# A graph network on one core: first layer ahead of the edge ranks, index work moved into the first blocks, padding rows scattered by GpSimd

## Chip, cores and metric

The kernel runs on one NeuronCore of a Trainium2 chip. The metric is the device time of one execution in microseconds (us). Engines are named TensorE (PE in the profile; PEld is its weight load), VectorE (DVE), ScalarE (ACT), GpSimd (POOL) and SyncE (SP), the last of which issues most DMA transfers.

## What is computed

Two graph layers follow each other on 512 nodes of 256 features, with 16,384 edges. The first carries nearly all of the work: three dense layers on every edge, then a sum over the edges of each source node, then a dense part on the nodes. The second layer is node attention, messages along the same edges, a feed-forward part and a gated unit.

```python
m = gelu(h_E @ m0_w + m0_b)          # 16384 x 512 -> 256
m = gelu(m @ m1_w + m1_b)            # 256 -> 256
m = gelu(m @ m2_w + m2_b)            # 256 -> 256
dh = segment_sum(m, src_idx, num_segments=512) / 30.0
h = layer_norm(h_V + dh)
d = gelu(h @ d0_w + d0_b); d = gelu(d @ d1_w + d1_b); d = d @ d2_w + d2_b
x = layernorm(x + layer_norm(h + d))
...
msg = x1[dst] * x1[src]
attn_out = segment_sum(msg, dst, num_segments=512)
```

## The kernel before

**Edge blocks.** The edges are taken in 32 blocks of 512 (`NBLK`, `BLK`). `layer_0(b, m)`, `layer_1(b)` and `layer_2(b)` are TensorE's three layers of block b. Every float32 product is made of three passes over values split into a rounded part and its rest (`x_hi`, `x_lo`): ScalarE rounds (`round_x`), VectorE subtracts (`rest_x`, `rest_w`, `rest_0`, `rest_1`). TensorE's order in block b is `layer_1(b)`, `layer_0(b + 1, 0)`, `layer_2(b)`, `layer_0(b + 1, 1)`. VectorE adds the last bias (`biased`), ScalarE applies the last gelu (`gelu_2`) into `m2`.

**Sorting the edges.** To sum over source nodes, the rows of `m2` are sorted by source group (128 nodes each, `NC` = 4 groups) through HBM. Blocks are taken in 8 sorts (`SORT_BLOCKS`: six of 4 blocks, two of 3). A sort owns a stretch of the HBM tensor `sorted_rows`, in which each group begins on a multiple of 128 rows. GpSimd writes the rows with indirect DMAs (L450, four of 128 rows for each block) at the addresses in `place`. For the last two blocks (`DIRECT`) no sort is made. Rows of `sorted_rows` that get no edge must hold -1 in their index columns, so SyncE first fills each sort's whole stretch from the tile `no_edge` (`fill`, L363), ahead of the scatters. `fill(0)` is issued behind the loads of blocks 0 to 2, the others in blocks 1, 5, 9 and so on to 25. GpSimd waits for the fill (`filled`) at the first block of a sort.

**Summing.** The sorted rows come back in chunks of 5 tiles of 128 rows (`reload(q)`, L374, into `sorted_raw`), from block 4 on. VectorE makes one-hot matrices of their index columns (`hot_src`, `hot_dst`; the latter's first one of a chunk stands between `rest_1(b, 0)` and `rest_1(b, 1)`), ScalarE and VectorE split the values (`round_sorted`, `rest_sorted`), and `sum_sorted(q)` adds them up on TensorE, 6 blocks behind (`LAG_SUM`).

**The index work ahead of it.** `group_edges` (VectorE) makes `group_hot`, the group of each edge as one-hot; `rank_edges` (TensorE, L1262 and L1264) counts with 17 matmuls how many edges of the same group stand ahead; `place_edges` (VectorE) turns that into addresses, group beginnings (`group_at`) and the group of each tile (`tile_group`). TensorE runs `rank_edges`, then 16 warming matmuls on the identity (`keep_warm`, L1317), then `layer_0(0, ...)`. Each engine carries out its program in the order in which it is written; there is no scheduler. All DMAs that SyncE issues share one queue, in the page q1. In block 26 SyncE loads the node weights of the next stage (`x_rows`, `d0_w`, and `d1_w` of 4 MB).

VectorE's order before block 0 was:

```python
group_edges()
for g in range(2):
    rest_w(g)
    rest_x(0, g)
rest_w(2)
rest_w(3)
place_edges()
rest_0(0, 0)
```

## Time and profile before

| | us |
|---|---|
| median of 3 timed runs | 628.16 (627.64 to 629.81) |
| the profiled execution | 624.47 |
| its span, first to last instruction | 622.7 |
| TensorE busy | 591.8 (95%) |
| VectorE busy | 458.0 (74%) |
| ScalarE busy | 366.5 (59%) |
| GpSimd busy | 193.1 (31%) |
| moved by DMA | 102.82 MB, of which 35.53 MB written to HBM |
| mean granted clock of TensorE | 0.994 |

The span runs from the first to the last instruction; the execution's own time is 1.8 us longer. TensorE's matmuls are pipelined, and each one's end is modelled, so differences of starts are read rather than durations. A wait is shown in brackets behind an instruction: how long its engine was idle ahead of it, and what released it. The granted clock is 1.00 at 2.4 GHz and 0.50 at 1.2 GHz.

### The profile page before, as it was taken

To read this page: it belongs to the slowest core of one execution; us is meant where nothing else is said; L and a number is where in the kernel's file an instruction comes from. 1 tells how busy PE (TensorE), PEld (TensorE's weight loads), DVE (VectorE), ACT (ScalarE), POOL (GpSimd) and SP (SyncE) were. 2 spreads that over 40 slices of the span, in tenths; PEclk is the share of its full clock that TensorE was granted. 3 is DMA by queue.
4 is the path that set the end of the run, shared out by engine and by line. 5 is a ranking of instruction groups with operands and counts; after the bars stand their busy time and mean duration, and the time that the engine had idled before them with its cause. 6 is when DMAs were issued, how large, how long until landed. Compare 5 with 4: busy or idle time off the path is not lost.

```text
span 622.7 us, 9161 instructions
## 1 busy us (share of the span) xinstructions
PE 591.8 (95%) x3273; PEld 507.7 (82%) x3273; DVE 458.0 (74%) x781; ACT 366.5 (59%) x554; POOL 193.1 (31%) x182
## 2 busy tenths in 40 slices
PE   4999999999999999999999989998789999999895
PEld 1888887898888888888888978888778889778673
DVE  4756577778778887787887869879546666778567
ACT  4667686776777767776777766663156352420341
POOL 3035345534554445543554344510000010100001
PEclk9999999999999999999999999999799999999999
DMA  7994399499479549739748994232021213000000
GB/s 245 286 280 168 116 284 321 122 274 288 146 229 304 192 128 280 254 108 284 241 153 232 354 397 147 80 119 86 1 102 68 101 44 136 1 0 2 0 1 34
DMA packets 51483, 102.82 MB, mean 165 GB/s; under 512 B 3568, under 2 KB 41328, under 8 KB 46960
## 3 DMA queue, kind: packets, MB, share of 16 engines
q1 hardware_dynamic: 45104, 86.04, 44.6%
q0 software_dynamic: 5760, 15.92, 7.7%
q8 instruction: 28, 0.46, 0.3%
q10 hardware_dynamic: 576, 0.28, 0.2%
q14 instruction: 15, 0.12, 0.1%
HBM read 66.69 MB, written 35.53 MB: 164 GB/s over the span
## 4 chain that ended last, share of the span: by engine, by line
PE 81%; DMA 9%; DVE 6%; issue 2%; ACT 2%; POOL 1%; SPq 0%; POOLq 0%; ACTq 0%; DVEq 0%
PE ps L1209 24%; PE ps L1245 8%; DMA sorted_raw<-sorted_rows 7%; PE ps L1391 7%; PE ps L1251 4%; PE ps L1227 4%; PE ps L1223 4%; PE ps L1222 4%; PE ps L1359 3%; PE ps L1290 3%; PE ps L1294 3%; PE ps L1292 3%; PE ps L1432 2%; PE ps L1317 2%; PE ps L1402 2%
## 5 line engine op out<-in xcount | busy, mean ns | idle before, releaser
L450 POOL DMA_INDIRECT sorted_rows<-m,place x120 | 163.1, 1359 | 211.3 <-ACT m L514 182.8
L497 ACT ACTIVATE m_hi<-ps,cols 128x512 fp32r<-128x512 f32 x128 | 88.3, 690 | 75.7 <-PE ps L1209 47.5
L772 DVE TENSOR_TENSOR m_lo<-m_out,m_hi 128x512 fp32r<-128x512 f32 x128 | 88.7, 693 | 59.1 <-ACT m_out L499 55.7
L1209 PE MATMUL ps<-x_hi,w_hi 128*128 128x512 f32 x256 | 100.2, 391 | 0.0
L1209 PE MATMUL ps<-x_lo,w_hi 128*128 128x512 f32 x256 | 100.1, 391 | 0.0
L1209 PE MATMUL ps<-x_hi,w_lo 128*128 128x512 f32 x256 | 99.8, 390 | 0.0
L499 ACT ACTIVATE m_out<-ps,cols 128x512 f32<-128x512 f32 x128 | 88.0, 688 | 0.0
L688 DVE TENSOR_TENSOR x_lo<-x_raw,x_hi 128x1024 fp32r<-128x1024 f32 x64 | 75.8, 1224 | 7.0 <-ACT x_hi L491 7.0
L1245 PE MATMUL ps<-w_lo,m_hi 128*128 128x256 f32 x256 | 64.2, 283 | 0.0
L1245 PE MATMUL ps<-w_hi,m_hi 128*128 128x256 f32 x256 | 64.0, 282 | 0.0
L491 ACT ACTIVATE x_hi<-x_raw 128x1024 fp32r<-128x1024 f32 x62 | 62.2, 1058 | 1.9 <-DMA x_raw<-in_edges_dram 1.9
L514 ACT ACTIVATE m<-m_in 128x512 f32<-128x512 f32 x64 | 39.5, 634 | 40.4 <-DVE m_in L785 40.4
L803 DVE TENSOR_SCALAR pack_hot<-iota,sorted_raw 128x256 fp32r<-128x256 f16 x144 | 53.4, 408 | 7.3 <-DMA sorted_raw<-sorted_rows 7.3
L1209 PEld LDWEIGHTS ps<-x_hi,w_lo 128*128 128x128 f32 x256 | 48.1, 188 | 10.3
L1209 PEld LDWEIGHTS ps<-x_hi,w_hi 128*128 128x128 f32 x256 | 48.2, 188 | 9.2
L1209 PEld LDWEIGHTS ps<-x_lo,w_hi 128*128 128x128 f32 x256 | 48.2, 188 | 8.8
L785 DVE TENSOR_TENSOR m_in<-ps,m2b 128x512 f32<-128x512 f32 x64 | 41.2, 686 | 19.1 <-PE ps L1251 19.1
L1245 PEld LDWEIGHTS ps<-w_lo,m_hi 128*128 128x128 f32 x256 | 49.0, 192 | 1.2
L1223 PE MATMUL ps<-m_hi,w_lo 128*128 128x512 f32 x128 | 50.0, 390 | 0.0
L1245 PEld LDWEIGHTS ps<-w_hi,m_hi 128*128 128x128 f32 x256 | 48.9, 191 | 1.2
L1222 PE MATMUL ps<-m_hi,w_hi 128*128 128x512 f32 x128 | 49.9, 390 | 0.0
L1290 PE MATMUL ps<-sorted_hi,src_hot 128*128 128x256 f32 x144 | 42.9, 298 | 5.8 <-issue 3.8
(208 smaller groups left out, 1140.7 us busy)
## 6 DMA issues: line engine op xcount, KB each, us to landing
x_raw<-in_edges_dram SPq DMA_DIRECT2D x31, 1024.0 KB, 7.3
sorted_raw<-sorted_rows SPq DMA_DIRECT2D x24, 647.5 KB, 5.2
sorted_rows<-no_edge SPq DMA_DIRECT2D x6, 2460.5 KB, 19.3
d_w<-in_d_dram SPq DMA_DIRECT2D x1, 4096.0 KB, 27.8
sorted_rows<-no_edge SPq DMA_DIRECT2D x2, 1942.5 KB, 17.0
sorted_raw<-sorted_rows SPq DMA_DIRECT2D x6, 518.0 KB, 4.0
rows<-in_rows_dram SPq DMA_DIRECT2D x1, 2176.0 KB, 8.3
d_w<-in_d_dram SPq DMA_DIRECT2D x2, 1024.0 KB, 11.4
```

Source lines behind the costliest of these rows:

```text
L450: pool.indirect_dma_start(out=sorted_d, out_offset=bass.IndirectOffsetOnAxis(ap=place[:, at:at + 1], axis=0), in_=m2[:, b % 2, t], in_offs ...
L491: nc.scalar.activation(x_hi[:, b % 2, K_HALF[h]], x_raw[:, b % 2, K_HALF[h]], ACT.Copy).then_inc(x_hi_done, 1)
L497: nc.scalar.activation(out_hi[:, m], ps[:, bank], ACT.Gelu, bias=col(bias, m)).then_inc(hi_signal, 1)
L499: nc.scalar.activation(m_out[:, m], ps[:, bank], ACT.Gelu, bias=col(bias, m)).then_inc(signal, 1)
L688: nc.vector.tensor_tensor(x_lo[:, b % 2, ks], x_raw[:, b % 2, ks], x_hi[:, b % 2, ks].bitcast(F32), ALU.subtract).then_inc(x_lo_done, 1)
L772: nc.vector.tensor_tensor(lo[:, m], m_out[:, m], hi[:, m].bitcast(F32), ALU.subtract).then_inc(done, 1)
L803: nc.vector.tensor_scalar(pack_hot[:, q % 2, t], iota[:, 0:2 * P], near, unit, ALU.is_equal, ALU.mult)
L1209: last = nc.tensor.matmul(out, left, right, start=(k == 0 and i == 0), stop=(k == KE - 1 and i == 2))
L1222: nc.tensor.matmul(out, w(1, k, m, w_hi), m0_hi[:, k], start=(k == 0), stop=False, skip_group_check=True)
L1223: nc.tensor.matmul(out, w(1, k, m, w_lo), m0_hi[:, k], start=False, stop=False, skip_group_check=True)
L1245: nc.tensor.matmul(out, m1_hi[:, k, e], part[:, at:at + H], stop=False, skip_group_check=True, start=(k == 0 and part is w_hi and t % 2 == 0))
L1290: nc.tensor.matmul(group_sum[:, g], hot, sorted_hi[:, q % 2, t], start=False, stop=False, skip_group_check=True)
```

## The change

It has five parts.

- **TensorE's start.** The warming matmuls come first, as soon as the identity is there; then `layer_0(0, 0)` and `layer_0(0, 1)`; `rank_edges` stands behind them, ahead of `layer_1(0)`.
- **VectorE's start.** The first halves of weights and input of block 0 are split ahead of `group_edges`.
- **Index work.** `place_edges` is cut into `count_groups` (block 0, behind the input of block 2), `place_edges` (end of block 0) and `group_tiles` (end of block 1).
- **Padding.** The eight fills are gone. A new `pad_rows` (VectorE, end of block 2) computes the addresses of the rows that get no edge, 384 for each sort, and GpSimd scatters `no_edge` into them: 24 indirect DMAs of 128 rows, two in each block from block 3 to 14, ahead of the block's own scatters. `reload` waits for a sort's three (`padded`) at its first chunk, the load of `d1_w` for all of them, `sum_sorted(0)` for their addresses.
- **Drain.** A `drain` of GpSimd follows its last scatter.

```diff
+PADS = NC - 1
...
+        FIRST_PADS = 3
...
-
-            def fill(s):
-                rows_s = sorted_d[s * TILES * P:(s * TILES + SORT_TILES[s]) * P].rearrange("(t p) f -> p t f", p=P)
-                all_rows = no_edge[:].rearrange("p (a f) -> p a f", a=1).to_broadcast([P, SORT_TILES[s], ROW])
-                sp.dma_start(rows_s, all_rows).then_inc(filled[s], 16)
 
...
@@ -368,6 +372,7 @@
                     past = SORT_FIRST[sort] + SORT_BLOCKS[sort]
                     for par in range(2):
                         sp.wait_ge(scattered[par], 64 * ((past + 1 - par) // 2))
+                    sp.wait_ge(padded[sort], 16 * PADS)
                 if q >= 2:
                     sp.wait_ge(sorted_ready, q - 1)
                 at = (sort * TILES + CHUNK * c) * P
...
             load_x(1)
             load_x(2)
-            sp.wait_ge(consts, 1)
-            fill(0)
             for b in range(NBLK):
                 if b + 3 < NBLK:
                     load_x(b + 3)
-                if b % 4 == 1 and b // 4 + 1 < SORTS:
-                    fill(b // 4 + 1)
                 if b == NBLK - 6:
                     sp.dma_start(x_rows[:].rearrange("p c f -> p (c f)"), x_rows_d).then_inc(early_loaded, 16)
                     sp.dma_start(d0_w[:].rearrange("p a b -> p (a b)"), d0_d).then_inc(early_loaded, 16)
-                    sp.wait_ge(placed, 1)
+                    for s in range(SORTS):
+                        sp.wait_ge(padded[s], 16 * PADS)
                     sp.dma_start(d1_w[:].rearrange("p a b -> p (a b)"), d1_d).then_inc(early_loaded, 16)
...
                 if b == 0:
                     pool.wait_ge(placed, 1)
                 pool.tensor_copy(m2[:, b % 2, :, H:ROW], edge_id[:, b * TB:(b + 1) * TB]).then_inc(ids_in, 1)
-                if b in SORT_FIRST:
-                    pool.wait_ge(filled[SORT_FIRST.index(b)], 16)
+                if b == FIRST_PADS:
+                    pool.wait_ge(pads_placed, 1)
+                for i in range(max(2 * (b - FIRST_PADS), 0), min(2 * (b - FIRST_PADS) + 2, PADS * SORTS)):
+                    rows_at = pad_place[:, i // PADS, i % PADS:i % PADS + 1]
+                    pool.indirect_dma_start(out=sorted_d, out_offset=bass.IndirectOffsetOnAxis(ap=rows_at, axis=0),
+                                            in_=no_edge[:], in_offset=None).then_inc(padded[i // PADS], 16)
                 pool.wait_ge(ids_in, b + 1)
                 for t in range(TB):
                     pool.wait_ge(gelu2, 2 * b + t // 2 + 1)
                     at = place_of(b, t)
                     pool.indirect_dma_start(out=sorted_d, out_offset=bass.IndirectOffsetOnAxis(ap=place[:, at:at + 1], axis=0),
                                             in_=m2[:, b % 2, t], in_offset=None).then_inc(scattered[b % 2], 16)
+            pool.drain()
...
-            def place_edges():
+            def count_groups():
 
                 totals = ps[:, CNT].rearrange("p (g s c) -> p g s c", g=NC, s=SORTS)
-                ranks = ps[:, CNT + 1].rearrange("p (g s c) -> p g s c", g=NC, s=SORTS)
                 dve.wait_ge(ranked, 1)
                 dve.wait_ge(consts, 2)
                 idx(nc.vector.tensor_reduce(group_n[:], totals, AX_X, ALU.add))
...
+                row_s = sort_row[:].rearrange("p (a s) -> p a s", a=1).to_broadcast([P, NC, SORTS])
+                idx(nc.vector.scalar_tensor_tensor(group_row[:], group_at[:], float(P), row_s, ALU.mult, ALU.add))
+                idx_wait()
+
+            def group_tiles():
+
                 one = slice(0, 1)
                 for g in (1, 2, 3):
...
-                row_s = sort_row[:].rearrange("p (a s) -> p a s", a=1).to_broadcast([P, NC, SORTS])
-                idx(nc.vector.scalar_tensor_tensor(group_row[:], group_at[:], float(P), row_s, ALU.mult, ALU.add))
                 idx_wait()
                 idx(nc.vector.tensor_tensor(tile_past[one, 0], tile_past[one, 0], tile_past[one, 1], ALU.add))
+                idx_wait()
+                idx(nc.vector.tensor_tensor(tile_group[one], tile_past[one, 0], tile_past[one, 2], ALU.add))
+
+            def place_edges():
+
+                ranks = ps[:, CNT + 1].rearrange("p (g s c) -> p g s c", g=NC, s=SORTS)
                 first = group_row[:].rearrange("p g (s a) -> p g s a", a=1).to_broadcast([P, NC, SORTS, COLS_SORT])
                 idx(nc.vector.tensor_tensor(rank[:], ranks, first, ALU.add))
                 idx_wait()
-                idx(nc.vector.tensor_tensor(tile_group[one], tile_past[one, 0], tile_past[one, 2], ALU.add))
                 idx(nc.vector.tensor_tensor(rank[:], rank[:], group_hot[:, :, :, COLS_SORT - 1:], ALU.mult))
...
                 idx_wait()
                 idx(nc.vector.tensor_reduce(place_f[:], rank[:].rearrange("p g s c -> p (s c) g"), AX_X, ALU.add))
                 idx_wait()
                 nc.vector.tensor_copy(place[:], place_f[:]).then_inc(placed, 1)
+
+            def pad_rows():
+
+                idx(nc.vector.tensor_copy(before_n[:, 0], group_n[:, 0]))
+                idx_wait()
+                for g in range(1, PADS):
+                    idx(nc.vector.tensor_tensor(before_n[:, g], before_n[:, g - 1], group_n[:, g], ALU.add))
+                    idx_wait()
+                idx(nc.vector.scalar_tensor_tensor(before_n[:], group_at[:, 1:], float(P), before_n[:], ALU.mult, ALU.subtract))
+                idx_wait()
+                each = [P, PADS, SORTS, PADS]
+                limit = before_n[:].rearrange("p g (s a) -> p g s a", a=1).to_broadcast(each)
+                rows_in = group_n[:, 1:].rearrange("p g (s a) -> p g s a", a=1).to_broadcast(each)
+                idx(nc.vector.tensor_tensor(pad_past[:], pad_no[:].to_broadcast(each), limit, ALU.is_ge))
+                idx(nc.vector.tensor_tensor(pad_row[:], pad_row[:],
+                                            group_n[:, 0].rearrange("p (s a) -> p s a", a=1).to_broadcast([P, SORTS, PADS]),
+                                            ALU.add))
+                idx_wait()
+                idx(nc.vector.tensor_tensor(pad_past[:], pad_past[:], rows_in, ALU.mult))
+                idx_wait()
+                idx(nc.vector.tensor_reduce(pad_n[:], pad_past[:].rearrange("p g s k -> p s k g"), AX_X, ALU.add))
+                idx_wait()
+                nc.vector.tensor_tensor(pad_place[:], pad_row[:], pad_n[:], ALU.add).then_inc(pads_placed, 1)
 
             def rest(hi, lo, signal, done, b, m):
 
@@ -840,13 +882,13 @@
                 into = count[:, 2 * r:2 * r + 2, far * H:(far + 1) * H]
                 nc.vector.tensor_tensor(into, into, field.rearrange("p (g n) -> p g n", g=2), ALU.add).then_inc(count_step, 1)
 
+            rest_w(0)
+            rest_x(0, 0)
+            rest_w(1)
             group_edges()
-            for g in range(2):
-                rest_w(g)
-                rest_x(0, g)
+            rest_x(0, 1)
             rest_w(2)
             rest_w(3)
-            place_edges()
             rest_0(0, 0)
             rest_x(1, 0)
             rest_x(1, 1)
...
@@ -857,6 +899,8 @@
                 if b + 2 < NBLK:
                     rest_x(b + 2, 0)
                     rest_x(b + 2, 1)
+                if b == 0:
+                    count_groups()
                 for s, first in enumerate(COUNTS_OUT_AT):
                     if first <= b < first + 4:
                         add_counts(s, (b - first) // 2, (b - first) % 2)
@@ -872,6 +916,12 @@
                 rest_0(b + 1, 0)
                 biased(b, 0)
                 biased(b, 1)
+                if b == 0:
+                    place_edges()
+                if b == 1:
+                    group_tiles()
+                if b == 2:
+                    pad_rows()
                 if q >= 0:
                     for t in range(2, CHUNK):
                         hot_dst(q, t)
@@ -1256,7 +1306,6 @@
             def rank_edges():
 
                 pe.wait_ge(group_ready, 1)
-                pe.wait_ge(ident_ready, 1)
                 flat = group_hot[:].rearrange("p g s c -> p (g s) c")
                 own = flat[:, :, COLS_SORT - 1:]
                 nc.tensor.matmul(ps[:, CNT], all_ones[:], own, start=True, stop=True)
@@ -1273,7 +1322,7 @@
 
                 sort, c, n = CHUNKS[q]
                 if q == 0:
-                    pe.wait_ge(placed, 1)
+                    pe.wait_ge(pads_placed, 1)
                     clear(SUM)
                     clear(SUM + 1)
                 if q == 0 or q - 1 in COUNT_AFTER:
@@ -1316,10 +1365,11 @@
                 for _ in range(products):
                     nc.tensor.matmul(ps[:, bank, 0:P], ident[:], ident[:], start=True, stop=True)
 
-            rank_edges()
+            pe.wait_ge(ident_ready, 1)
             keep_warm(16, 0)
             layer_0(0, 0)
             layer_0(0, 1)
+            rank_edges()
             for b in range(NBLK - 1):
                 layer_1(b)
                 layer_0(b + 1, 0)
```

VectorE before its first block, in the kernel before from the end of `group_edges` on (names: `w_lo`, `x_lo` are the rests of weights and input, `part_i`, `group_hot` and `edge_id` come from `group_edges`, `group_n` is the first of `place_edges`):

```order
L726 CAST direct_src<-src_i 128x8
L727 CAST iota<-iota_i 128x512
L728 CAST edge_id<-part_i 128x128
L729 CAST edge_id<-part_i 128x128
L730 TENSOR_SCALAR edge_id<-part_i 128x128
L693 TENSOR_TENSOR w_lo<-w_raw,w_hi 128x512 [waits w_hi_done]
L688 TENSOR_TENSOR x_lo<-x_raw,x_hi 128x1024 [waits x_hi_done]
L693 TENSOR_TENSOR w_lo<-w_raw,w_hi 128x512 [waits w_hi_done]
L688 TENSOR_TENSOR x_lo<-x_raw,x_hi 128x1024 [waits x_hi_done]
L693 TENSOR_TENSOR w_lo<-w_raw,w_hi 128x512 [waits w_hi_done] x2
L739 TENSOR_REDUCE group_n<-ps 128x32 [waits consts,ranked]
```

and VectorE's first rows in the changed kernel:

```order
L704 TENSOR_TENSOR w_lo<-w_raw,w_hi 128x512 [waits w_hi_done]
L699 TENSOR_TENSOR x_lo<-x_raw,x_hi 128x1024 [waits x_hi_done]
L704 TENSOR_TENSOR w_lo<-w_raw,w_hi 128x512 [waits w_hi_done]
L722 TENSOR_SCALAR part_i<-src_i 128x128 [waits idx_loaded]
L723 TENSOR_SCALAR part_i<-src_i 128x128
L724 TENSOR_SCALAR part_i<-dst_i 128x128
L725 TENSOR_SCALAR part_i<-dst_i 128x128
L733 TENSOR_SCALAR group_hot<-part_i 128x6x16 [waits idx_step,consts]
```

and, VectorE still, behind the middle of `group_edges`:

```order
L738 CAST iota<-iota_i 128x512
L739 CAST edge_id<-part_i 128x128
L740 CAST edge_id<-part_i 128x128
L741 TENSOR_SCALAR edge_id<-part_i 128x128
L699 TENSOR_TENSOR x_lo<-x_raw,x_hi 128x1024 [waits x_hi_done]
L704 TENSOR_TENSOR w_lo<-w_raw,w_hi 128x512 [waits w_hi_done] x2
L814 TENSOR_TENSOR m_lo<-m_out,m_hi 128x512 [waits gelu0]
```

The first two rests of the weights and the first half of the input's have moved ahead of the edge groups, and m_lo follows the weights directly, with no index work between.

VectorE at the end of block 0 in the changed kernel (`m_in` is `biased`, `m_lo` behind it is `rest_0(1, 1)`):

```order
L814 TENSOR_TENSOR m_lo<-m_out,m_hi 128x512 [waits gelu1]
L814 TENSOR_TENSOR m_lo<-m_out,m_hi 128x512 [waits gelu0]
L827 TENSOR_TENSOR m_in<-ps,m2b 128x512 [waits l2_done] x2
L780 TENSOR_TENSOR rank<-ps,group_row 128x512
L782 TENSOR_TENSOR rank<-rank,group_hot 128x512 [waits idx_step]
L784 TENSOR_REDUCE place_f<-rank 128x128 [waits idx_step]
L786 CAST place<-place_f 128x128 [waits idx_step]
L814 TENSOR_TENSOR m_lo<-m_out,m_hi 128x512 [waits gelu0]
L699 TENSOR_TENSOR x_lo<-x_raw,x_hi 128x1024 [waits x_hi_done] x2
```

The four operations from `rank` to `place` have come in between `m_in` and `m_lo`, which stood next to each other.

SyncE's queue from the load of block 1 on, before:

```order
L358 DMA x_raw<-in_edges_dram 128x2048
L358 DMA x_raw<-in_edges_dram 128x2048 [waits x_lo_done]
L363 DMA sorted_rows<-no_edge 128x19x259 [waits consts]
L358 DMA x_raw<-in_edges_dram 128x2048 [waits x_lo_done] x2
L363 DMA sorted_rows<-no_edge 128x19x259
L358 DMA x_raw<-in_edges_dram 128x2048 [waits x_lo_done] x3
L374 DMA sorted_raw<-sorted_rows 128x5x259 [waits scattered1,scattered0]
L358 DMA x_raw<-in_edges_dram 128x2048 [waits x_lo_done]
L363 DMA sorted_rows<-no_edge 128x19x259
L374 DMA sorted_raw<-sorted_rows 128x5x259
```

and now:

```order
L367 DMA x_raw<-in_edges_dram 128x2048
L367 DMA x_raw<-in_edges_dram 128x2048 [waits x_lo_done] x6
L379 DMA sorted_raw<-sorted_rows 128x5x259 [waits padded0,scattered1,scattered0]
L367 DMA x_raw<-in_edges_dram 128x2048 [waits x_lo_done]
L379 DMA sorted_raw<-sorted_rows 128x5x259
L367 DMA x_raw<-in_edges_dram 128x2048 [waits x_lo_done]
```

The fills (L363) are out of the queue, one of them from directly ahead of the second reload, and the first reload has a third thing to wait for.

## Rows read from the trace of the kernel before

**Rows 1.** TensorE's waits: waited for, us in total, times, longest
```profile
PE ps L1262 <- DVE group_hot L722: 8.4, 1, 8.4
PE ps L1251 <- DVE m_lo L772: 3.4, 2, 2.5
```

**Rows 2.** Timeline of TensorE's start: start us, us, engine line operation
```profile
8.37 0.61 PE L1262 MATMUL ps<-group_hot,all_ones 128*128 128x512 bf16 x1 [8.37 <-DVE group_hot L722]
9.21 5.79 PE L1264 MATMUL ps<-group_hot,all_ones 128*128 128x512 bf16 x15
14.83 3.73 PE L1317 MATMUL ps<-ident 128*128 128x128 f32 x32
18.32 0.47 PE L1209 MATMUL ps<-x_hi,w_hi 128*128 128x512 f32 x1
...
23.87 0.39 PE L1222 MATMUL ps<-m_hi,w_hi 128*128 128x512 f32 x1
...
26.85 0.39 PE L1209 MATMUL ps<-x_hi,w_hi 128*128 128x512 f32 x1
```

**Rows 3.** Timeline of the other engines at the start, and VectorE in block 0
```profile
3.34 0.28 POOL L430 TENSOR_SCALAR_AFFINE_SELECT ident<-ident 128x128 f32<-128x128 f32 x1
...
6.49 1.06 ACT L546 ACTIVATE x_hi<-x_raw 128x1024 fp32r<-128x1024 f32 x1 [1.89 <-DMA x_raw<-in_edges_dram]
6.67 0.23 DVE L711 TENSOR_SCALAR part_i<-src_i 128x128 int32<-128x128 int32 x1 [6.67 <-DMA dst_i<-in_dst_dram]
...
9.04 0.68 DVE L693 TENSOR_TENSOR w_lo<-w_raw,w_hi 128x512 fp32r<-128x512 f32 x1
9.64 1.22 DVE L688 TENSOR_TENSOR x_lo<-x_raw,x_hi 128x1024 fp32r<-128x1024 f32 x1
...
15.03 0.69 DVE L739 TENSOR_REDUCE group_n<-ps 128x32 f32<-128x512 f32 x1 [1.23 <-PE ps L1264]
...
18.03 0.67 DVE L760 TENSOR_TENSOR rank<-ps,group_row 128x512 f32<-128x512 f32 x1
...
20.80 0.23 DVE L767 CAST place<-place_f 128x128 int32<-128x128 f32 x1
...
36.70 0.69 DVE L772 TENSOR_TENSOR m_lo<-m_out,m_hi 128x512 fp32r<-128x512 f32 x1 [3.00 <-ACT m_out L499]
```

**Rows 4.** Timeline of the two holes, VectorE and TensorE
```profile
99.00 0.41 DVE L803 TENSOR_SCALAR pack_hot<-iota,sorted_raw 128x256 fp32r<-128x256 f16 x1 [2.55 <-DMA sorted_raw<-sorted_rows]
100.07 0.74 PE L1251 MATMUL ps<-w_hi,m_lo 128*128 128x256 f32 x4 [0.92 <-DVE m_lo L772]
...
372.04 0.41 DVE L803 TENSOR_SCALAR pack_hot<-iota,sorted_raw 128x256 fp32r<-128x256 f16 x1 [4.75 <-DMA sorted_raw<-sorted_rows]
373.11 0.74 PE L1251 MATMUL ps<-w_hi,m_lo 128*128 128x256 f32 x4 [2.51 <-DVE m_lo L772]
```

**Rows 5.** Chain of waits around the two holes: start us, us, what
```profile
77.68 21.30 DMA sorted_raw<-sorted_rows
...
349.18 22.83 DMA sorted_raw<-sorted_rows
```

**Rows 6.** The page's DMA issues, fills: count, KB each, median us to landing
```profile
sorted_rows<-no_edge SPq DMA_DIRECT2D x6, 2460.5 KB, 19.3
...
sorted_rows<-no_edge SPq DMA_DIRECT2D x2, 1942.5 KB, 17.0
```

**Rows 7.** The page's costliest groups, scatters: busy us, mean ns, idle before
```profile
L450 POOL DMA_INDIRECT sorted_rows<-m,place x120 | 163.1, 1359 | 211.3 <-ACT m L514 182.8
```

**Rows 8.** Timeline of GpSimd, its first operation behind the last scatter
```profile
453.12 0.10 POOL L462 MEMSET norm_cols<- 128x4 f32 x1 [44.95 <-PE ps L1309]
```

**Rows 9.** The tail: TensorE's timeline; ten us: PE, PEld, DVE, ACT, POOL, PEclk, DMA
```profile
439.50 0.38 PE L1290 MATMUL ps<-sorted_hi,src_hot 128*128 128x256 f32 x1 [1.99 <-issue]
...
440.00:450.00 10.00, 8.65 (x52) 8.36 (x52) 5.55 (x12) 0.00 (x0) 0.00 (x0) 0.66 0.01 2
```

**Rows 10.** Durations of x_lo subtractions on VectorE: ns min/median/max
```profile
L688 DVE TENSOR_TENSOR x_lo<-x_raw,x_hi x64: 1218/1223/1281, 9.6 to 393.3; 128x1024 fp32r<-128x1024 f32 x64
```

15 lines of the change are left out of this document (13 added, 2 removed).

## Prediction

> **What bounds the kernel now.** The first view to read is TensorE's list of waits: it says whether TensorE, the busiest engine by far, ever stands still. It does so very little. Once for 8.4 us in front of its first matmul, twice (3.4 us together) for a VectorE result of the edge loop, and a few times in the tail [rows 1]. Between 27 and 99 us there is no wait at all, so the edge loop advances at TensorE's pace, and only three places can pay: the start and those two holes.
>
> The start is read from the timeline [rows 2]. TensorE first works at 8.37 us, on the rank matmuls: 15 of them take 5.79 us, 0.39 apart. Sixteen warming matmuls follow at 14.83, the first layer of block 0 at 18.32, its second layer at 23.87, and block 1's first layer at 26.85. That last time is my anchor: from there TensorE runs on without a wait. From 18.32 to 23.87 lie 24 matmuls, 0.231 us apart.
>
> The holes are at 100.07 (0.92 us) and 373.11 (2.51 us). In both VectorE had stood idle directly before, 2.55 and 4.75 us, waiting for `sorted_raw` from HBM [rows 4]. The chain of waits gives the reason: reloads under way for 21.30 and 22.83 us [rows 5]. The page's DMA issues show what shares the queue: every fill writes 2.46 MB (1.94 for the last two) and takes 19.3 or 17.0 us to land [rows 6]. Fill 2 is issued by SyncE directly ahead of the reload that came late at 99 us; fill 7 is issued in block 25, ahead of the node weights (a 4 MB load among them) and of the reload that was late at 372.
>
> **The start, part by part.** The identity is made by 3.62 us (3.34 + 0.28) [rows 3], so the warming matmuls can begin there. They took 3.5 us before (14.83 to 18.32); if TensorE starts at its lower level they take up to twice that, so they end between 7.1 and 10.6.
>
> VectorE's new order: the first half of x_hi ends at 7.55 (6.49 + 1.06); x_lo takes 1.14 by start-to-start at 9.64 and its 1.22, w_lo 0.60 (9.04 to 9.64), so both are done at about 9.3. `group_edges` took 2.37 (6.67 to 9.04) and now runs from 9.3 to 11.7. The second x_lo half ends 1.22 later, at 12.95 [rows 3]. TensorE does the first six matmuls ahead of that and waits for this half. From 12.95 there are 18 matmuls of the first layer, 17 rank matmuls and 12 of the second layer: 47, at 0.231, are 10.9 us. Block 1's first layer starts at 23.8 instead of 26.85: **3.0 us gained**.
>
> The unknown here is the rank matmul. It has the same 512 columns as the others yet came at 0.39 on average [rows 2]. Either TensorE was at its lower level, or the data (16-bit, in short strided pieces) sets 0.39. I take the first, because those matmuls were TensorE's first work of the run, and the same columns pass in 0.231 just behind. If the data sets it, 17 matmuls cost 2.6 us more and 0.4 is left of the gain. The Trainium skill, "TensorE: Matmul & The Clock Gate", Part 1, says that the array is at half rate by default and that activity releases it; by that the first reading is right and the whole 3.0 stands.
>
> **The index work on VectorE.** `count_groups` took at most 3.0 us (15.03 to 18.03, with four `tile_past` operations that are moved away). It now stands in block 0 behind the x_lo pair of block 2; VectorE comes to it while TensorE has rank, second-layer and first-layer matmuls queued. `place_edges` took 3.00 us (18.03 to 20.80, + 0.23), now less one small step (`tile_group`). Its new place, behind the second `biased` of block 0, is one where VectorE idled 3.00 us for m_out [rows 3]. It fits, with nothing to spare; GpSimd's first scatter waits for its result, and nothing else does before block 3. `group_tiles` (5 operations) and `pad_rows` (9, of 24 to 72 columns) sit in the same hole of blocks 1 and 2, and at some 0.2 us each they are under 2 us. Cost 0; were this cover gone, up to 3 us in block 0 and 2 in each of the others would show.
>
> **The fills.** Eight transfers, 18.6 MB (6 x 2.46 + 2 x 1.94), go; 24 scatters of 128 rows come, 24 x 0.133 = 3.2 MB. The late reloads no longer have a fill ahead: at 99 us the reload needed 2.55 us less out of 21.30 while the fill ahead of it took 19.3; at 372 it needed 4.75 less (2.51 for TensorE), and fill 7's transfer took 17.0. Both holes close: **0.9 + 2.5 = 3.4 us gained**. Next late at 373 would be the reload behind the 4 MB load; it has to come only 4.75 us sooner, and the fill was about a sixth of the bytes ahead of it in the same queue, so this hole may close in part. Between 0 and 3.4 is possible; I take 3.4, since a fill's many small rows cost the queue more than their bytes.
>
> **GpSimd's pads.** Each indirect scatter costs 1.36 us, and GpSimd idles 182.8 us waiting for ScalarE's output, 6.1 in each of the 30 blocks that it scatters [rows 7]. Two pads (2.7 us) fit in every block from 3 to 14. Only sort 0 is close: its third pad comes in block 4, behind block 3's scatters, so the first reload may be issued some 2 us later; VectorE first needs it a block later. SyncE queues block 8's input behind that wait, which has a block to spare too. The wait of d1_w for all pads is met in block 14, ten blocks ahead.
>
> **The drain.** GpSimd has nothing to do for 44.95 us behind its last scatter [rows 8], so the drain costs 0 unless it lasts longer than that.
>
> **Sum.** 3.0 + 3.4 = 6.4 us. The profiled execution took 624.47 us, which makes 618.1 by its own time. The three timed runs have the median 628.16, 3.7 above it; I subtract from that: **621.8 us**. If those 3.7 us are longer holes of the same sort, they go too (618.1).
>
> **Rivals.**
> - *Rank matmuls are slow by their data.* Gain 0.4 + 3.4 = 3.8, 624.4 us. For it: the 15 stayed at 0.39 on average over 5.79 us, long enough for a clock to have risen earlier. Chance 0.08.
> - *The reloads stay late*, since the node weights or the late pads hold them, wholly or mostly. Gain 3.0, 625.2 us. The second hole supports it, the first speaks against it. Chance 0.12.
> - *TensorE's clock falls in the new gap* between the warming matmuls and 12.95, or at another point of the tail. The profile shows one such fall: the matmuls began again at 439.50 after an idle 1.99 us, and in the ten us from 440 the mean granted clock is 0.66 [rows 9]; between the levels of 2.4 and 1.2 GHz that is 3.4 us of full-speed work lost. Against it: the four matmuls behind the 2.51 us hole take 0.74 us, as those behind the 0.92 us one do [rows 4]. 625.2 us. Chance 0.08. The Trainium skill, same page, Part 1, says that idle time brings the lower rate back; whether this gap does, no row can say.
> - *The pads hold up VectorE* (ends slower). Place: blocks 3 to 14, where each pad's descriptors are made while VectorE subtracts. Price: 24 x 1.36 = 32.6 us if all of it is passed on to TensorE; the change turns slower by over 0.3% once more than 6.4 + 1.9 = 8.3 us, a quarter, is passed on, giving 630 us and up, 654 at worst. Against it: 64 x_lo subtractions, beside 120 scatters, all took 1.218 to 1.281 us [rows 10], so VectorE is not held today. Chance 0.05. The Trainium skill, "SBUF — State Buffer", section "SBUF: two separate sides", says that a VectorE operation with two SBUF inputs and a GpSimd one exclude each other; by it this rival would be likely, and the narrow durations disagree for VectorE's side.
> - *Nothing changes that can be measured*: both gains are absorbed by a later wait of the tail. Chance 0.07, 627.5 us.
>
> **Numbers.** Forecast 0.60. A measurement of this kernel tells about 0.3% (1.9 us) from no change; the forecast and the first three rivals all gain over 1.9 us, 0.88 together. Same 0.07, slower 0.05. The range goes down to 616.5 (618.1 and the spread of some 1.5 us that the three runs show) and up to 626.0 (the rivals at 625.2 with the little that they may vary).
>
> **What would show it.** Right: TensorE's first matmul at about 3.7 us, one short wait before about 13, rank matmuls near 0.23 apart, block 1's first layer at about 23.8; no wait for m_lo near 96 and 365; reloads there landing in under 15 us. Wrong: rank matmuls at 0.4; a granted clock of 0.5 between 10 and 25 us; VectorE waiting for `sorted_raw` at its first use; x_lo subtractions over 1.3 us in blocks 3 to 14. A time above 626.3 would refute the forecast.

## The result, and the profile after

| | before | changed |
|---|---|---|
| median of the runs, us | 628.49 (627.64 to 629.81, 4) | 618.64 (616.26 to 621.67, 4) |
| profiled execution, us | 624.47 | 616.26 |
| its span, us | 622.7 | 614.2 |
| TensorE busy, us | 591.8 | 591.0 |
| GpSimd busy, us | 193.1 | 219.6 |
| HBM written, MB | 35.53 | 19.62 |

The ratio is 0.9846 (95% interval 0.9808 to 0.9884): faster by 1.5%. The median of 618.64 lies between two pairs of runs, 616.26 and 616.35, and 620.93 and 621.67. In a second comparison, on one chip with several of the experiments below, the changed kernel took 617.96 us (616.24 to 620.88, 6 runs) against 631.62 (19 runs), ratio 0.9801 (0.9773 to 0.9829). The changed kernel stayed where it was; it was the kernel before that came out 3 us higher.

TensorE's waits, in the order of the list. The waits for `group_hot` (8.4 us) and `m_lo` (3.4 us) of [rows 1] are gone, and what is new is short:

```profile
PE ps L1366 <- POOL ident L432: 3.7, 1, 3.7
PE ps L1339 <- issue: 3.0, 3, 2.0
...
PE ps L1259 <- DVE x_lo L699: 1.1, 1, 1.1
```

TensorE's timeline of the start, which answers to [rows 2]: the warming matmuls come first, one wait for the second `x_lo` half, the rank matmuls (L1311, L1313) behind block 0's first layer, and block 1's first layer at 23.69 us:

```profile
3.68 6.55 PE L1366 MATMUL ps<-ident 128*128 128x128 f32 x32 [3.68 <-POOL ident L432]
9.98 0.48 PE L1259 MATMUL ps<-x_hi,w_hi 128*128 128x512 f32 x1
...
12.76 0.49 PE L1259 MATMUL ps<-x_hi,w_hi 128*128 128x512 f32 x1 [1.13 <-DVE x_lo L699]
...
16.99 0.41 PE L1311 MATMUL ps<-group_hot,all_ones 128*128 128x512 bf16 x1
17.23 0.39 PE L1313 MATMUL ps<-group_hot,before_me 128*128 128x512 bf16 x1
17.46 3.64 PE L1313 MATMUL ps<-group_hot,all_ones 128*128 128x512 bf16 x15
20.74 0.60 PE L1272 MATMUL ps<-m_hi,w_hi 128*128 128x512 f32 x1
...
23.69 0.39 PE L1259 MATMUL ps<-x_hi,w_hi 128*128 128x512 f32 x1
```

VectorE's timeline of the same stretch, beside [rows 3]. `count_groups` begins at 24.62 and ends at 26.65, `place_edges` runs from 30.61 to 33.39; the reader is to see that TensorE's line above has no wait that names either:

```profile
7.37 1.23 DVE L699 TENSOR_TENSOR x_lo<-x_raw,x_hi 128x1024 fp32r<-128x1024 f32 x1 [2.02 <-ACT x_hi L557]
...
11.48 1.22 DVE L699 TENSOR_TENSOR x_lo<-x_raw,x_hi 128x1024 fp32r<-128x1024 f32 x1
...
24.62 0.69 DVE L749 TENSOR_REDUCE group_n<-ps 128x32 f32<-128x512 f32 x1
...
26.46 0.19 DVE L762 SCALAR_TENSOR_TENSOR group_row<-group_at,sort_row 128x32 f32<-128x32 f32 x1
26.69 1.29 DVE L814 TENSOR_TENSOR m_lo<-m_out,m_hi 128x512 fp32r<-128x512 f32 x2
...
33.16 0.23 DVE L786 CAST place<-place_f 128x128 int32<-128x128 f32 x1
```

VectorE at the places of the two holes [rows 4]. It no longer waits for `sorted_raw`, here or at the second place:

```profile
93.36 0.41 DVE L845 TENSOR_SCALAR pack_hot<-iota,sorted_raw 128x256 fp32r<-128x256 f16 x1
...
363.01 0.41 DVE L845 TENSOR_SCALAR pack_hot<-iota,sorted_raw 128x256 fp32r<-128x256 f16 x1
```

GpSimd: its scatters by tile, which answers to [rows 7], and its first operation behind the last one [rows 8]. The 24 padding scatters (L454) cost 1.24 us each in the median, between 59.5 and 197.9 us; the wait for ScalarE falls from 182.8 to 132.5 us (columns of the first two lines: ns min/median/max, first and last start):

```profile
L460 POOL DMA_INDIRECT sorted_rows<-m,place x120: 956/1168/2398, 34.3 to 400.2; - x120
...
L454 POOL DMA_INDIRECT sorted_rows<-no_edge,pad_place x24: 960/1241/1528, 59.5 to 197.9; - x24
...
  ACT m L525: 132.5, 29
```

GpSimd's timeline at the end of its idle stretch. The new drain is not shown in it as work; the trace's own record of it ends at 410.0 us, 8.8 us behind the last scatter's end, so 34 us of the 43 are still free:

```profile
444.56 0.10 POOL L473 MEMSET norm_cols<- 128x4 f32 x1 [43.36 <-PE ps L1358]
```

TensorE's timeline of the tail, and the ten us in which the clock fell (PE, PEld, DVE, ACT, POOL, PEclk, DMA), as in [rows 9]; then the `x_lo` durations [rows 10]:

```profile
417.34 0.38 PE L1339 MATMUL ps<-sorted_hi,src_hot 128*128 128x256 f32 x1 [2.01 <-DVE sorted_lo L850]
432.62 0.57 PE L1339 MATMUL ps<-sorted_hi,src_hot 128*128 128x256 f32 x1 [2.04 <-issue]
```

```profile
430.00:440.00 10.00, 7.46 (x47) 6.97 (x47) 7.93 (x17) 2.31 (x3) 0.00 (x0) 0.83 0.01 2
```

```profile
L699 DVE TENSOR_TENSOR x_lo<-x_raw,x_hi x64: 1217/1224/1254, 7.4 to 386.4; 128x1024 fp32r<-128x1024 f32 x64
```

**Where 8.5 us of span went.** Start: 26.85 to 23.69, 3.16. Up to the first sum of the tail (420.24 to 413.27) it is 6.97: the start's 3.16, the holes' 3.43, and 0.38 that is left over for the loop. From there to GpSimd's last operation another 1.6 us, since the clock fell for less long (0.66 in ten us before, 0.83 now). Behind that operation nothing: 3.1 us in both.

### The profile page after: what moved, and what is told of

Its sections match the earlier page's. It is cut to its first block, busy times and chain, and to the rows that moved or that the text cites. A ratio compares the mean times of both kernels' runs of the same rounds, so it can differ in the third digit from the quotient of the medians.

```text
span 614.2 us, 9200 instructions
## 1 busy us (share of the span) xinstructions
PE 591.0 (96%) x3273; PEld 509.0 (83%) x3273; DVE 460.1 (75%) x790; ACT 366.4 (60%) x554; POOL 219.6 (36%) x208
## 3 DMA queue, kind: packets, MB, share of 16 engines
HBM read 66.69 MB, written 19.62 MB: 141 GB/s over the span
## 4 chain that ended last, share of the span: by engine, by line
PE 90%; DVE 6%; ACT 2%; issue 1%; DMA 1%; POOLq 0%; POOL 0%; SPq 0%; DVEq 0%
PE ps L1259 28%; PE ps L1295 10%; PE ps L1441 7%; PE ps L1301 5%; PE ps L1277 5%; PE ps L1273 5%; PE ps L1272 5%; PE ps L1409 3%; PE ps L1339 3%; PE ps L1341 3%; PE ps L1343 3%; PE ps L1482 2%; PE ps L1452 2%; PE ps L1366 1%; PE ps L1471 1%
## 5 line engine op out<-in xcount | busy, mean ns | idle before, releaser
L460 POOL DMA_INDIRECT sorted_rows<-m,place x120 | 162.0, 1350 | 160.5 <-ACT m L525 132.5
L470 POOL TENSOR_TENSOR norm_cols<-norm_cols 128x2 f32<-128x2 f32 (+1 forms) x14 | 9.5, 676 | 113.1 <-DVE norm_cols L970 113.1
```

The costliest lines, as they stand in the source:

```text
L460: pool.indirect_dma_start(out=sorted_d, out_offset=bass.IndirectOffsetOnAxis(ap=place[:, at:at + 1], axis=0), in_=m2[:, b % 2, t], in_offs ...
```

## The experiments

The table holds one profiled execution of each kernel, in us from the span's start: block 1's first layer, TensorE's waits for `m_lo` (the holes), the first sum behind the loop, the first warming matmul behind the last sum, GpSimd's last operation, and the span. From the fifth column to the sixth it is 165.4 us in every kernel, so the table has all that differs.

| kernel | block 1 | holes | sum | warming | GpSimd's last | span |
|---|---|---|---|---|---|---|
| before | 26.85 | 0.92, 2.51 | 420.24 | 454.23 | 619.62 | 622.7 |
| changed | 23.69 | none | 413.27 | 445.67 | 611.06 | 614.2 |
| start only | 23.81 | 0.81, 2.58 | 418.41 | 453.76 | 619.16 | 622.3 |
| pads only | 26.79 | none | 416.28 | 450.46 | 615.85 | 625.5 |
| no drain | 23.86 | none | 413.33 | 447.17 | 612.58 | 622.2 |
| early fills | 26.24 | 4.28 elsewhere | 422.45 | 454.74 | 620.13 | 623.2 |
| changed, again | 23.87 | none | 413.28 | 445.61 | 611.00 | 614.1 |
| drain only | 25.84 | 2.27, 5.42 | 427.62 | 461.84 | 627.25 | 630.4 |
| start and drain | 23.74 | 3.67, 4.56 | 425.56 | 459.43 | 624.82 | 627.9 |
| pads and drain | 25.58 | none | 415.01 | 447.38 | 612.78 | 615.9 |
| warm tail | 25.31 | none | 414.67 | 451.17 | 616.57 | 619.7 |
| 12 pads, no drain | 23.87 | 2.89 | 418.03 | 451.92 | 617.34 | 627.4 |
| drain in block 14 | 25.66 | none | 415.11 | 450.40 | 615.79 | 621.5 |
| 120 scatters, 12 of them pads | 25.38 | 2.69 | 417.78 | 450.13 | 615.54 | 624.7 |

### First comparison: the parts without the drain

The kernel before took 624.84 us here (621.01 to 627.82, 35 runs).

**The start alone.** The order of the changed kernel on VectorE and TensorE, with the fills of the kernel before, no pads and no drain:

```diff
-                for i in range(max(2 * (b - FIRST_PADS), 0), min(2 * (b - FIRST_PADS) + 2, PADS * SORTS)):
...
+                if b in SORT_FIRST:
+                    pool.wait_ge(filled[SORT_FIRST.index(b)], 16)
...
-            pool.drain()
```

> The part of the change at the start alone (warming matmuls and first layer ahead of the ranks, index work in blocks 0 and 1); the eight fills stay as they were, no pads, no drain. Theory: the gain of the start is 3.2 us (block 1's first layer at 23.7 instead of 26.85) and both holes for late reloads stay, 0.9 and 2.5 us, so TensorE still waits for m_lo twice, 3.4 us together; time about 3.2 below the kernel before. Rival (earlier start only makes the loop wait longer for the fills): under 1.5 us gained, the holes wider by the rest. Rival (the fills slowed more than the two holes): well over 3.2 left to the pads.

Measured: 623.82 us (12 runs), ratio 0.9983 (0.9964 to 1.0003). The mark of block 1 is 3.0 us early, as it should be, but TensorE's waits have both holes still, and the window around the second has the clock at 0.83 (PEclk, the third number from the end):

```profile
PE ps L1301 <- DVE m_lo L816: 3.4, 2, 2.6
```

```profile
365.00:375.00 10.00, 7.42 (x40) 6.21 (x38) 6.04 (x11) 3.94 (x6) 1.31 (x1) 0.83 0.81 315
```

The kernel before, with a hole of 2.51 us at 373.11 us, has a granted clock of 1.00 in the same ten us. So the 3.0 us gained at the start are there in the marks; 1.2 of them are lost again by the first sum (418.41 against 420.24) and 1.4 more by the warming matmuls (453.76 against 454.23). The median keeps 1.0, and the interval includes no change.

**The pads alone.** The changed kernel with the old order at the start and without the drain:

```diff
-                if b == 0:
-                    count_groups()
...
-            pool.drain()
...
+            rank_edges()
             keep_warm(16, 0)
             layer_0(0, 0)
             layer_0(0, 1)
-            rank_edges()
```

> The padding part alone: fills out, pads by GpSimd in blocks 3 to 14, their addresses made in block 2; the start as in the kernel before, no drain. Theory: both holes close, 3.4 us gained, block 1's first layer still at 26.85. Rival (fills also slowed the steady loop or the start): over 4.5 us gained. Rival (pads hold VectorE up): under 2.5 gained and x_lo subtractions over 1.3 us in blocks 3 to 14.

Measured: 624.94 us, ratio 1.0012 (0.9993 to 1.0031). Both holes are gone and TensorE's marks are 3.8 us ahead of the kernel before (450.46 against 454.23), yet the span is 2.8 us longer. All of that lies behind GpSimd's last operation.

**The change without its drain.** One line is taken out:

```diff
-            pool.drain()
```

> The changed kernel without its drain of GpSimd behind the last scatter. Theory: GpSimd is idle there for 45 us, so the time is that of the changed kernel (616 to 622, two groups by where the clock falls) within 0.2%. Rival: the drain is worth something in the tail (the tail is 1.6 us shorter than before in the changed kernel's profile); then this kernel is slower than the changed one by 1.5 us or more in every run.

Measured: 625.81 us (622.45 to 628.36, 12 runs), ratio 1.0017 (0.9989 to 1.0045). My prediction priced the drain at nothing, and without it nothing is left of the change against the kernel before. (The changed kernel itself was not among this comparison's kernels; its 616 to 622 us are from two others.) The timelines show where. GpSimd's last operation here, of a span of 622.2 us, and VectorE's and SyncE's work behind it:

```profile
612.58 0.54 POOL L469 TENSOR_TENSOR norm_cols<-norm_cols 128x1 f32<-128x1 f32 x1 [3.76 <-DVE norm_cols L969]
613.16 0.41 DVE L980 TENSOR_SCALAR hat<-res,mean_var,norm_cols 128x256 f32<-128x256 f32 x1 [0.66 <-POOL norm_cols L469]
613.60 0.33 SPq L416 DMA_DIRECT2D out_dram<-hat  x1
```

and in the kernel before, of 622.7 us:

```profile
619.62 0.54 POOL L459 TENSOR_TENSOR norm_cols<-norm_cols 128x1 f32<-128x1 f32 x1 [3.76 <-DVE norm_cols L920]
```

From this operation to the end are 9.6 us here and 3.1 there. The last output transfer is issued at 613.60 in the kernel without the drain; nothing but GpSimd's own end is left after it. Each of the fourteen traces ends with a drain on GpSimd that the kernel does not write, and the trace's record of it lasts 9.41 us here, 1.32 in the kernel before and 0.65 in the changed one. It does not wait for data: the last of GpSimd's scatters has landed at 403.50 us by the trace, 209 us earlier.

**Fills two blocks earlier.** The kernel before, with its second fill issued at the start, behind the first, and every later one two blocks sooner:

```diff
             fill(0)
+            fill(1)
...
-                if b % 4 == 1 and b // 4 + 1 < SORTS:
-                    fill(b // 4 + 1)
+                if b % 4 == 3 and b // 4 + 2 < SORTS:
+                    fill(b // 4 + 2)
```

> The kernel before with each fill issued two blocks earlier (fill 1 with fill 0, the others in blocks 3, 7, ... 23 instead of 5, 9, ... 25), the same bytes. If the holes come only from a fill standing in the queue directly ahead of a late reload: the hole at 100 us closes or moves to block 4's first reload, the one at 373 shrinks from 2.5 to under 1 us, and the time falls by 2 to 3.4 us. If the bytes as such are the cause (the queue is full over dozens of us): both stay, and the time is that of the kernel before within 1 us.

Measured: 626.46 us, ratio 1.0011 (0.9988 to 1.0034). Both holes are gone, and a new one of 4.28 us is there, with the clock at 0.55 in the five us from 45. TensorE's timeline, and ScalarE's, which waits 5.90 us for the edge features:

```profile
44.63 0.58 PE L1246 MATMUL ps<-w_hi,m_hi 128*128 128x256 f32 x1 [4.28 <-ACT m_hi L498]
```

```profile
42.00 2.00 ACT L492 ACTIVATE x_hi<-x_raw 128x1024 fp32r<-128x1024 f32 x2 [5.90 <-DMA x_raw<-in_edges_dram]
```

So the fills' place in the transfers decides where a hole is. This one move of theirs moved the hole; the kernels here that have none are those without fills.

### Second comparison: the same parts with the drain

The kernel before took 631.62 us here (628.89 to 634.73, 19 runs). The last three kernels have one line more than the kernel before, the start alone and the pads alone:

```diff
                                             in_=m2[:, b % 2, t], in_offset=None).then_inc(scattered[b % 2], 16)
+            pool.drain()
             norms = [0]
```

**The changed kernel, again**, without an edit.

> The changed kernel again, so that it stands on one chip beside its parts. Theory (start 3.2 us, holes 3.4 us, and a drain that takes GpSimd's closing 6.5 us out of the end where that end is the long one): some 7 to 8 us under the kernel before, 616 to 618 us, and the stretch from GpSimd's last operation to the end of the span is 3.1 us. Rival (the version without the drain was slow for another reason of that chip): near 624 us here too.

Measured: 617.96 us, ratio 0.9801; 3.1 us from GpSimd's last operation to the end.

**The drain alone**, in the kernel before.

> The kernel before with one line more, the drain behind GpSimd's last scatter; start, fills and order stay. Theory (the drain empties GpSimd's queue of software DMAs while it has 45 us to spare, so that its closing drain finds nothing): the end behind GpSimd's last operation is 3.1 us in the profile, and the median falls by what share of the kernel before's executions have the long end, 0 to 6 us; the timed runs are then narrower than the 7 us of the kernel before. My costing in the prediction: the drain is worth 0, ratio 0.998 to 1.002, spread unchanged.

Measured: 631.65 us (12 runs), ratio 1.0000 (0.9977 to 1.0024), and the stretch behind GpSimd's last operation is 3.1 us, as without a drain. So the drain pays nothing by itself: the kernel before has no long closing drain to take away. Of the kernels here only those with pads need it. This profile shows also what the kernel before loses in a comparison where it takes 631 us. TensorE's waits, VectorE's timeline at both holes, the reloads in the chain of waits, and windows of five us behind the holes:

```profile
PE ps L1252 <- DVE m_lo L773: 7.7, 2, 5.4
```

```profile
99.41 0.41 DVE L804 TENSOR_SCALAR pack_hot<-iota,sorted_raw 128x256 fp32r<-128x256 f16 x1 [3.90 <-DMA sorted_raw<-sorted_rows]
...
376.84 0.41 DVE L804 TENSOR_SCALAR pack_hot<-iota,sorted_raw 128x256 fp32r<-128x256 f16 x1 [7.65 <-DMA sorted_raw<-sorted_rows]
```

```profile
76.74 22.64 DMA sorted_raw<-sorted_rows
...
351.07 25.74 DMA sorted_raw<-sorted_rows
```

```profile
100.00:105.00 5.00, 4.53 (x15) 3.82 (x16) 5.00 (x10) 1.91 (x3) 0.89 (x1) 0.66 0.99 374
...
375.00:380.00 5.00, 2.10 (x7) 1.91 (x8) 3.16 (x6) 1.27 (x1) 0.00 (x0) 0.68 0.95 368
380.00:385.00 5.00, 5.00 (x18) 3.76 (x18) 3.08 (x6) 2.18 (x4) 3.13 (x2) 0.64 0.25 66
```

The reloads take 1.3 and 2.9 us more than in [rows 5], the holes are 7.7 us in place of 3.4, and the clock falls behind each of them.

**The start with the drain**, fills kept.

> The start alone with the drain, fills kept. If the drain's gain adds to the start's: the end behind the last GpSimd operation is 3.1 us instead of the 9.6 us seen without it where long, and the median is 2 to 6 us under the start alone (623.8 us), so 618 to 622 us; the waits for the reloads stay at 97 and 370 us. If the drain is worth nothing: 623 to 624 us.

Measured: 627.33 us (8 runs), ratio 0.9935 (0.9911 to 0.9959). Against the drain alone that is 4.3 us for the start, where the marks show 2.1 (25.84 to 23.74; the old start was itself a microsecond earlier here than in [rows 2]) and the span 2.5; the rest of the 4.3 is not explained. The holes are 8.2 us.

**The pads with the drain**, old start.

> The padding rows with the drain, old start. If the drain is what the pads alone lacked: the median falls from 624.9 to about 619 to 621 us, and the end is 3.1 us. If the 24 small scatters cost the time by themselves (a busier DMA queue): it stays at 625 us. The whole change should be 3 us faster than this one, by the start.

Measured: 620.49 us (617.85 to 620.75, 6 runs), ratio 0.9823 (0.9797 to 0.9849): 11.1 us, most of the change. In the profiles the span falls by 14.5 against the drain alone. The changed kernel's start takes another 2.5 us off the median and 1.8 off the span.

### Third comparison: what the closing drain depends on, and the tail's clock

The kernel before took 625.40 us (20 runs).

**Warming products in the tail.** The changed kernel with eight products ahead of three sums:

```diff
             sum_sorted(NQ - 5)
+            keep_warm(8, 1)
             sum_sorted(NQ - 4)
...
             for q in range(NQ - 3, NQ):
+                keep_warm(8 if q < NQ - 1 else 0, 1)
                 sum_sorted(q)
```

> The whole change with 8 small products on TensorE (into a bank that is free there) ahead of the sums of chunks NQ-4, NQ-3 and NQ-2, where it stands idle for 2.02, 2.02 and 0.88 us. Theory (the clock falls behind these idle stretches, at 430 to 440 us in the profile and in other places in the executions near 621 us): the granted clock stays at 1.00 from 10 us to the last product, 1.7 us less than the 616.3 us of the profile, so near 614.8 us, and the executions spread by less than 2 us. Rival (the products delay the sums that follow as much as they save, or the fall stays): 616 to 618 us as before.

Measured: 620.39 us (618.64 to 621.78, 9 runs), ratio 0.9929 (0.9906 to 0.9953). The changed kernel was not in this comparison; in two others it had medians of 618.64 and 617.96 us, so no improvement shows. The clock is better (0.993 to 0.999 over the runs, against 0.988 to 0.994), and the time is not: the best run here has 0.999 and took 618.64 us, the changed kernel's best 0.994 and 616.24. TensorE's timeline:

```profile
416.55 1.95 PE L1366 MATMUL ps<-ident 128*128 128x128 f32 x16
419.16 0.38 PE L1339 MATMUL ps<-sorted_hi,src_hot 128*128 128x256 f32 x1 [0.66 <-issue]
...
433.81 1.95 PE L1366 MATMUL ps<-ident 128*128 128x128 f32 x16
436.44 0.38 PE L1339 MATMUL ps<-sorted_hi,src_hot 128*128 128x256 f32 x1 [0.69 <-issue]
440.70 0.58 PE L1339 MATMUL ps<-sorted_hi,src_hot 128*128 128x256 f32 x1 [2.21 <-issue]
```

After the products TensorE still stands 0.66, 0.69 and 2.21 us. In the program the fetch of the group numbers (`tile_group`) stands between the products and the sum, and its load begins at 433.59 us, just ahead of the second group of products; so it passes only partly beside them. From the first sum to the warming matmuls it is 36.5 us, against 32.4 in the changed kernel. The expected 614.8 us was a miss.

**Twelve pads, no drain.** The kernel without the drain, with pads for sorts 0 to 3 only and SP's fills for the others:

```diff
-                for i in range(max(2 * (b - FIRST_PADS), 0), min(2 * (b - FIRST_PADS) + 2, PADS * SORTS)):
+                for i in range(max(2 * (b - FIRST_PADS), 0), min(2 * (b - FIRST_PADS) + 2, PADS * 4)):
...
+                if b % 4 == 1 and 4 <= b // 4 + 1 < SORTS:
+                    fill(b // 4 + 1)
```

> The change without its drain, and with padding scatters for the first four sorts only, 12 in place of 24, the other four sorts filled by SP as before: 132 scatters in all, where 120 showed a closing stretch of 3.1 us and 144 one of 9.6 us. If the length of GpSimd's closing drain grows with their number: some 6 us. If it jumps somewhere: 3.1 or 9.6 us. The second reload hole (5th sort, filled by SP) may be there again with 2 to 5 us, the first not.

Measured: 629.62 us (6 runs), ratio 1.0088 (1.0055 to 1.0120): slower than the kernel before. The stretch behind GpSimd's last operation is 10.1 us. The first hole is gone and the second is back with 2.89 us: each hole goes with its own half of the fills.

**The drain in block 14** in place of behind the last scatter:

```diff
                                             in_=m2[:, b % 2, t], in_offset=None).then_inc(scattered[b % 2], 16)
+                if b == 14:
+                    pool.drain()
-            pool.drain()
```

> The change with its drain moved ahead, behind block 14's scatters; GpSimd then has 60 scatters behind it to the end. If what counts is what has gathered since the last drain: closing stretch 3.1 us. If it is the number of all scatters, or the lack of a drain at the end: 9.6 us. The drain itself waits there for the block's scatters to land; GpSimd has 4 to 5 us idle a block, and a wait of some 8 us would show as later scatters in block 15, and could show as a wait on TensorE through the m2 buffers; expected none, or under 2 us.

Measured: 621.77 us (12 runs), ratio 0.9941 (0.9918 to 0.9965). The closing stretch is 5.8 us, between the two expectations. The trace's record of the drain lasts 14.34 us in its new place, but it begins ahead of the block's last three scatters; GpSimd stands 8.92 us behind them, and TensorE shows no wait that comes from it.

### Fourth comparison: number or kind

**120 scatters, twelve of them pads.** The kernel with twelve pads, with the scatters of blocks 16 to 18 left out, so that the rows of three blocks are missing from its sums:

```diff
+        DROP = (16, 17, 18)
...
+                    if b in DROP:
+                        continue
```

> As the kernel with 12 padding scatters and no drain, but the 12 scatters of blocks 16 to 18 are left out (the rows of three blocks stay out of the sums), so that GpSimd issues 120 in all, as in the kernel before, and of these 12 are padding. If the length of the closing drain is a matter of how many scatters there are: 1.3 us as in the kernel before, 3.1 us from GpSimd's last operation to the end. If it is something about the padding scatters themselves (a table of places of their own, two at a block's start): 9 to 10 us as with 132 and 144, and 9.6 us to the end.

Measured: 628.98 us (12 runs), ratio 1.0056 (1.0030 to 1.0083) to a kernel before at 626.07 us. The stretch is 9.1 us. With the same number of scatters as the kernel before, the closing drain is still the long one, so their number alone does not set it.

All drains of GpSimd that the traces record, behind the one of 0.18 us at the start:

| kernel | scatters, of them pads | drain in the kernel, us | closing drain, us | to the end, us |
|---|---|---|---|---|
| before; start only; early fills | 120, 0 | none | 1.32 to 1.33 | 3.1 |
| drain only; start and drain | 120, 0 | 8.35; 8.03 | 0.65 | 3.1 |
| pads only; no drain | 144, 24 | none | 9.41 | 9.6 |
| 12 pads, no drain | 132, 12 | none | 9.90 | 10.1 |
| 120 scatters, 12 of them pads | 120, 12 | none | 8.92 | 9.1 |
| drain in block 14 | 144, 24 | 14.34 | 5.56 | 5.8 |
| changed, twice; pads and drain; warm tail | 144, 24 | 13.88 to 13.89 | 0.65 | 3.1 |

A record of a drain in the kernel begins ahead of the last scatters, so it overstates what the drain takes. By its end it can be compared: without pads it comes 0.4 us after the last scatter has landed (418.86 after 418.48; 416.43 after 416.06), with pads 6.3 to 6.5 us after (410.01 after 403.50, 411.76 after 405.51). So the pads lengthen this drain too, by about 6 us, and the time is not that of transfers on their way.

## Why the prediction was right, and where it was not

Predicted 621.8 us, in a range of 616.5 to 626.0; measured 618.64, inside it. The number came out partly by luck: the sum lacks two terms of 6.5 us that cancel.

**The start (3.0 us).** Right to a tenth in the profile: first matmul at 3.68, one wait that ends at 12.76 (12.95 predicted), rank matmuls some 0.23 us apart, block 1's first layer at 23.69 (23.8 predicted). The rank matmuls therefore were slow before by the clock at TensorE's first work, not by their data; that rival is refuted. The trace of the kernel before says the same when the fifteen of [rows 2] are divided at 13.8 us: eleven of them take 4.86 us, so that 0.93 is left for the other four.

```profile
9.21 4.86 PE L1264 MATMUL ps<-group_hot,all_ones 128*128 128x512 bf16 x11
```

By their single starts they come 0.43 us apart up to 13.90 us, and 0.23 from there on. That time varies too: it is 13.7 to 13.9 us in two profiles of the old start (block 1 at 26.85 and 26.79 us) and 11.2 to 12.0 in three (25.58 to 26.24). So 3.0 us is the difference to the late ones; in the second comparison the marks give 1.7 and 2.1.

The new start has bad executions of its own. In three of nine profiles with the new start the granted clock falls in and behind the wait for `x_lo` (2.1 to 2.5 us long there, 1.1 to 2.1 in the six others), and block 1 begins at 25.3 to 25.7 us. The window of the warm tail kernel:

```profile
15.00:20.00 5.00, 5.00 (x18) 3.22 (x17) 1.16 (x2) 4.97 (x8) 0.00 (x0) 0.76 0.36 152
```

So the rival "the clock falls in the new gap", to which I gave 0.08, is real in three of the nine profiles, and it costs about 1.6 us when it comes (block 1 at 25.45 us in the mean, against 23.81). The Trainium skill, "TensorE: Matmul & The Clock Gate", Part 1, says that idle time brings the lower rate back; these three agree. In the six others a wait at the same place had no such fall, but these were the shorter waits, if only by 0.03 us between 2.11 and 2.14.

**The holes (3.4 us).** Right in kind: both went, and by the reason given. The kernel with half of the fills keeps exactly the hole whose fill it keeps. In the changed kernel's second profile the reloads at the two places land after at most 10.8 and 15.2 us, in place of 21.30 and 22.83; the sign that I had set was 15. That many small rows are what makes a fill dear was not tried. The size was that of one execution. In another comparison the same holes cost 7.7 to 8.2 us, and 4.7 more by the clock behind them: from block 1 to the first sum the drain-only kernel takes 401.8 us and the changed one 389.4, of which 7.7 are waits; the granted clocks of the three windows above (0.66, 0.68, 0.64, each over five us) give an estimate of 5.1 for the rest. I had written that the 3.7 us between the profiled execution and the median might be longer holes that "go too (618.1)". The measured 618.64 and the profile of the drain-only kernel both speak for this: what varies in the kernel before seems to be the very thing that the change removes, so the saving should have been subtracted from the profiled execution, not from the median. It is argued and not shown, since no execution of the kernel before near 628 us was profiled; and from profile to profile the saving was 8.2 us, not 6.4, mostly by the 1.6 us of the tail below.

**The index work, the pads and VectorE (0).** Right. No wait of TensorE names `group_n`, `place` or `tile_group`, and `x_lo` took 1.217 to 1.254 us over the whole run. The exclusion of which the Trainium skill speaks ("SBUF — State Buffer", section "SBUF: two separate sides") does not show in these durations, with 24 scatters more than before.

**The drain (0).** This step failed. "The drain costs 0" is true of what it costs, and I asked only that. What it saves was never asked: the pads make GpSimd's closing drain 8 us longer (9.41 against 1.32), of which 6.5 reach the end of the span, and the drain behind the last scatter takes them back where GpSimd has 43 us to spare. Two terms of 6.5 us and opposite sign were missing from the sum, so it came out right by luck. Without the drain the ratio was 1.0017: "nothing changes that can be measured" was one line away, and I had not given it to that cause. The Trainium skill, "VectorE: DVE Perf Modes", section "The DRAIN you can't avoid", says of the drains that stand ahead of and behind every kernel that they are a constant of about 12 ns on all engines. The traces disagree for GpSimd's closing one: 0.65 to 9.90 us.

**The tail.** The rival that names another fall of the clock there holds in both directions: the changed kernel's profile gained 1.6 us in the tail, and the one of the kernel without the drain, with the same marks up to 413 us, lost 1.5 of them (447.17 against 445.67) by a second fall. The changed kernel's four first runs lie in two pairs, 616.3 at a mean granted clock of 0.994 and 621.3 at 0.988. The profile is of the first pair. A fall more would explain part of that; it was not seen, and stays open.

## What to carry to other kernels

A program's end is part of its time, and it belongs to no line of the kernel. If GpSimd issues scatters, read the stretch from its last operation to the end of the span, and where that is long, try a drain behind the last scatter, if the engine is idle there anyway. And if a kernel's runs lie above its profiled execution, ask first whether what the change removes is what varies; then take the saving from the execution in which it was read.

## What the runs showed of the hardware

- GpSimd's closing drain takes 1.3 us behind 120 scatters whose places come from one table, and 8.9 to 9.9 us where 12 or 24 padding scatters are among them, also at 120 in all, and 209 us after the last scatter has landed. A drain in the kernel makes it 0.65 us, if it is the last thing before the tail; from block 14 it leaves 5.56. Pads differ from the others in several ways (their own semaphores, a table and a source of their own), and which of them counts was not tried.
- Idle stretches of nearly the same length had different clocks: 2.51 us at 373 us without a fall (granted clock 1.00), 2.58 us at 370 with one (0.83 over ten us). That is part of why the same edit, the new start, gave 1.0 us in one comparison and 4.3 in another; the rest is open.
- The kernel before had medians of 624.84, 625.40, 626.07, 628.49 and 631.62 us in five comparisons, two of the five (626.07 and 631.62) on the same chip. Longer reloads and wider holes go with the slowest in the profiles; what makes them so is not known.
